# A fused GRU, attention, conditioned attention and expert network on one core: a second bank for the query-key product, a second bank for turned rows, and two pieces of a step in another order

## The reference

```python
xn = _rms_norm(x, g_norm) * (1.0 + scale) + shift      # scale, shift from emb @ W_emb
qkv = xn @ W_qkv                                       # 256 -> 3 x 256
q, k, v = ...                                          # 16 heads of 16
q, k = _rms_norm(q, g_q), _rms_norm(k, g_k)            # over each head's 16 numbers
logits = einsum('bhqd,bhkd->bhqk', q, k) * d ** (-0.5)
attn = softmax(logits)
o = einsum('bhqk,bhkd->bhqd', attn, v)
return o + o @ W_out
```

## Time and profile before

| | us |
|---|---|
| time of three runs, median | 1084.39 |
| lowest and highest | 1083.53, 1085.08 |
| the profiled execution's own time | 1083.47 |
| its span in the trace | 1081.3 |

### The profile page before, as it was taken

One profiled execution on the slowest core, in us unless ns is written; L12 is line 12 of the kernel. 1 busy time (PEld: TensorE's weight loads), 2 busy tenths in 40 slices (PEclk: granted clock), 3 DMA queues, 4 the chain that ended last, 5 costly groups with the idle time before them and its releaser, 6 DMA issues. The chain is left out here.

```text
span 1081.3 us, 33994 instructions
## 1 busy us (share of the span) xinstructions
PE 951.9 (88%) x13386; PEld 674.3 (62%) x13386; DVE 666.0 (62%) x2544; ACT 546.5 (51%) x1792; POOL 539.6 (50%) x1245
## 2 busy tenths in 40 slices
PE   3989999999999998679999999576985999999997
PEld 3777777777777777548888887444444444444443
DVE  5866666666666666677777777746855445454554
ACT  4544444444444444447777777566762333333432
POOL 1266666666666666615555553285002555555551
PEclk8555555555555555579999999988997999999999
DMA  6100000000000000020000100100000111112111
GB/s 267 42 4 4 3 4 3 4 3 3 4 4 3 4 3 4 2 81 31 31 31 31 31 2 2 35 3 2 1 1 18 35 60 58 51 51 68 51 51 39
DMA packets 9017, 30.28 MB, mean 28 GB/s; under 512 B 1446, under 2 KB 3112, under 8 KB 8492
## 3 DMA queue, kind: packets, MB, share of 16 engines
q1 hardware_dynamic: 8876, 28.32, 7.8%
HBM read 27.27 MB, written 1.05 MB: 26 GB/s over the span
## 5 line engine op out<-in xcount | busy, mean ns | idle before, releaser
L423 POOL COPY gp<-hq 128x16 f16<-128x16 f16 x256 | 69.1, 270 | 174.5 <-DVE hq L413 174.5
L306 ACT ACTIVATE r_scan<-gr 128x8 f32<-128x8 f32 x256 | 46.6, 182 | 180.3 <-PE gr L218 180.3
L432 POOL TENSOR_TENSOR q_part<-q_raw,q_part 128x64 f16<-128x64 f32 x238 | 111.6, 469 | 19.2
L398 DVE TENSOR_REDUCE z_sum<-gz 128x8 f32<-128x16 f32 x256 | 44.8, 175 | 120.6 <-PE gz L218 120.0
L218 PEld LDWEIGHTS gr<-hq,w_two 128*128 128x128 f16 x1024 | 47.4, 107 | 115.0 <-DVE hq L408 109.9
L218 PE MATMUL gr<-hq,w_one 128*128 128x4 f16 x2048 | 117.6, 166 | 0.0
L273 PE MATMUL gq<-gp,wq_part 128*128 128x64 f16 x1428 | 114.4, 237 | 0.0
L218 PE MATMUL gr<-hq,w_two 128*128 128x4 f16 x1024 | 68.7, 171 | 51.6 <-DVE hq L408 28.8
L924 POOL TENSOR_SCALAR probs<-probs,rinv 128x128 f32<-128x128 f32 (+1 forms) x128 | 53.0, 427 | 119.5 <-DVE rinv L820 119.5
L430 POOL CAST q_part<-q_raw 128x64 f16<-128x64 f32 x238 | 108.6, 456 | 0.0
L218 PEld LDWEIGHTS gr<-hq,w_one 128*128 128x128 f16 x2048 | 94.1, 103 | 0.0
(11 more groups left out here) (257 smaller groups left out, 2687.8 us busy)
## 6 DMA issues: line engine op xcount, KB each, us to landing
wf_ffn<-in_wf SPq DMA_DIRECT2D x28, 448.0 KB, 3.3
raw_attn<-in_pairs SPq DMA_DIRECT2D x8, 770.0 KB, 4.4
shared<-in_wq SPq DMA_DIRECT2D x1, 2056.0 KB, 12.3
xT<-in_xT SPq DMA_DIRECT2D x1, 1024.0 KB, 7.7
x<-in_xr SPq DMA_DIRECT2D x1, 1024.0 KB, 6.6
out<-fin SPq DMA_DIRECT2D x4, 256.0 KB, 2.5
whh<-in_whh SPq DMA_DIRECT2D x1, 768.0 KB, 4.7
wih<-in_wih SPq DMA_DIRECT2D x1, 768.0 KB, 6.8
```

The source lines that it names most:

```text
L306: nc.scalar.activation(r_scan[:, 2::3], R[bp][:, k * 8:(k + 1) * 8], ACT.Sigmoid, scale=1.0 / GS).then_inc(t_in, 1)
L398: nc.vector.tensor_reduce(z_sum[:], Z[bp][:, k * 16:(k + 1) * 16] .rearrange("p (m q) -> p m q", q=2), AX.X, ALU.add).then_inc(z_sum_ready, 1)
L423: nc.gpsimd.tensor_copy(gp[:, :, :, :, t].rearrange("p q j b -> p q (j b)"), hq[:, nxt, :, 2::3]).then_inc(h_stored, 1)
L432: nc.gpsimd.tensor_tensor(q_part[:, 1, h, :, :, c], src, q_part[:, 0, h, :, :, c], ALU.subtract).then_inc(q_split, 1)
```

## The change

It does four things, all in `adaln_block`.

1. The query-key product alternates between two banks (`qk_banks`), odd tiles in the old one, even tiles in `other32`. The product of tile t waits for `qk_ready` of tile t - 2.
2. A second bank for turned rows, `turn[1]`, which is the same memory as `other32`, is used alternately with `turn[0]` from the q rows of tile 6 to the k rows of tile 7, that is k rows of tile 6 and q rows of tile 7. After that it is the fifth bank for scores and weights.
3. Scores and weights therefore have 3 banks in turn in steps 4 to 7, 4 in steps 8 and 9 (`v_bank` is added), and 5 from step 10 on.
4. On TensorE `values` stands ahead of `batch_product`; and the shifted rows of a batch's second tile are turned (TensorE) and copied (ScalarE) after the first of a step's two units, not at the step's end.

```diff
-        bk = [... nc.psum_tensor(f"cb{i}", [P, HALF], F32) for i in range(7)]
-        turn = ctx.enter_context(nc.psum_tensor("turn", [P, 2 * HALF], FP16))
-        v_bank, x_bank, qk_bank = bk[4], bk[5], bk[6]
+        free_bank = [... for i in range(3)]
+        v_bank, x_bank, qk_bank = [... for i in range(3, 6)]
+        turn = [ctx.enter_context(nc.psum_tensor(f"turn{i}", [P, 2 * HALF], FP16)) for i in range(2)]
+        turn32, other32 = turn[0][:].bitcast(F32), turn[1][:].bitcast(F32)
+        qk_banks = (other32, qk_bank)
+        bk = free_bank + [v_bank, other32]
...
-            at = n % 4 if t < C0 else n % 5
+            at = n % (3 if t < TILES else 4 if t < TILES + 2 else 5)
...
+        two = [turn_of["q", TILES - 2], turn_of["k", TILES - 1]]
+        last_turn = [None, None]
+        for n, use in enumerate(turns):
+            at = (n - two[0]) % 2 if two[0] <= n <= two[1] else 0
+            turn_bank[use], turn_before[use], last_turn[at] = turn[at], last_turn[at], n
...
             def free_turn(kind, n):
-                at = turn_of[kind, n]
-                if at:
-                    pe.wait_ge(turn_read, at)
+                if turn_before[kind, n] is not None:
+                    pe.wait_ge(turn_read, turn_before[kind, n] + 1)
+                elif turn_bank[kind, n] is turn[1]:
+                    pe.wait_ge(qk_ready, TILES - 1)
...
             def freed(kind, n):
+                at = place[kind, n]
                 if before[kind, n]:
                     kind, n = before[kind, n]
                     pe.wait_ge(mx_done if kind == "score" else exp_done, n + 1)
+                elif at == 3:
+                    pe.wait_ge(v_done, TILES)
+                elif at == 4:
+                    pe.wait_ge(turn_read, last_turn[1] + 1)
...
-                    if t:
-                        pe.wait_ge(qk_ready, t)
-                    projected(qk_bank[:], t, slice(0, 2 * D), qk_psum)
+                    if t >= 2:
+                        pe.wait_ge(qk_ready, t - 1)
+                    projected(qk_banks[t % 2], t, slice(0, 2 * D), qk_psum)
...
                     if n == 0:
-                        if ("y", t // 4 - 3) in turn_of and t % 4 == 3 and t >= 15:
-                            batch_product(t // 4 - 3)
                         if 1 <= g <= QUADS:
                             values(g - 1)
+                        if t % 4 == 3 and t >= 15:
+                            batch_product(t // 4 - 3)
+                        b = (t - S0 - 4) // 4
+                        if t % 4 == 0 and 0 <= b < B:
+                            pe.wait_ge(shift_lo, b * TC + 2)
+                            rows_turned("shifted", q_rows, b * TC + 1)
...
-                b = (t - S0 - 4) // 4
-                if t % 4 == 0 and 0 <= b < B:
-                    pe.wait_ge(shift_lo, b * TC + 2)
-                    rows_turned("shifted", q_rows, b * TC + 1)
...
                     if n == 0 and 1 <= g <= QUADS:
                         raw(g - 1)
+                    b = (t - S0 - 4) // 4
+                    if n == 0 and t % 4 == 0 and 0 <= b < B:
+                        rows("shifted", qT, b * TC + 1)
```

More of the change, by code:

```diff
@@ L1021, in adaln_block @@
         oT = sb("oT2", [P, J, NT])
-        bk = [ctx.enter_context(nc.psum_tensor(f"cb{i}", [P, HALF], F32)) for i in range(7)]
-        turn = ctx.enter_context(nc.psum_tensor("turn", [P, 2 * HALF], FP16))
-        turn32 = turn[:].bitcast(F32)
-        v_bank, x_bank, qk_bank = bk[4], bk[5], bk[6]
+        free_bank = [ctx.enter_context(nc.psum_tensor(f"cb{i}", [P, HALF], F32))[:] for i in range(3)]
+        v_bank, x_bank, qk_bank = [ctx.enter_context(nc.psum_tensor(f"cb{i}", [P, HALF], F32))[:]
+                                   for i in range(3, 6)]
+        turn = [ctx.enter_context(nc.psum_tensor(f"turn{i}", [P, 2 * HALF], FP16)) for i in range(2)]
+        turn32, other32 = turn[0][:].bitcast(F32), turn[1][:].bitcast(F32)
+        qk_banks = (other32, qk_bank)
+        bk = free_bank + [v_bank, other32]
         o_bank = (x_bank, qk_bank)
@@ L1069, in weights_at @@
             return n if 0 <= n < len(weight_units) else None
-        uses, bank, before = [], {}, {}
+        uses, bank, place, before = [], {}, {}, {}
         for t in range(STEPS):
@@ L1078, in adaln_block @@
         for n, (kind, unit, t) in enumerate(uses):
-            at = n % 4 if t < C0 else n % 5
-            bank[kind, unit], before[kind, unit], last[at] = bk[at], last[at], (kind, unit)
-        turns = []
+            at = n % (3 if t < TILES else 4 if t < TILES + 2 else 5)
+            bank[kind, unit], place[kind, unit] = bk[at], at
+            before[kind, unit], last[at] = last[at], (kind, unit)
+        turns, turn_bank, turn_before = [], {}, {}
         for t in range(STEPS):
@@ L1129, in rows_turned @@
                 for hp in range(HP):
-                    mm = pe.transpose(turn[:, hp * P:(hp + 1) * P],
+                    mm = pe.transpose(turn_bank[kind, i][:, hp * P:(hp + 1) * P],
                                       rows[:, i, 2 * hp:2 * hp + 2, :].rearrange("p h n -> p (h n)"),
@@ L1262, in rows @@
                 nc.scalar.activation(dst[:, :, tile_cols(i)],
-                                     turn[:].rearrange("p (h t) -> p h t", h=HP),
+                                     turn_bank[kind, i][:].rearrange("p (h t) -> p h t", h=HP),
                                      ACT.Copy).then_inc(turn_read, 1)
@@ L1278, in exponentials @@
                     nc.scalar.activation(pT[:, n // 2 % 2, n % 2 * 2 + e].rearrange("p k t -> p (k t)"),
-                                         bank["weight", 2 * n + e][:], ACT.Exp,
+                                         bank["weight", 2 * n + e], ACT.Exp,
                                          scale=scale).then_inc(exp_done, 1)
@@ L1304, in _ @@
                         act.wait_ge(ss2_ready, t)
-                    nc.scalar.activation(sq[:], qk_bank[:], ACT.Square).then_inc(sq_ready, 1)
+                    nc.scalar.activation(sq[:], qk_banks[t % 2], ACT.Square).then_inc(sq_ready, 1)
                 if 2 <= t < TILES + 2:
@@ L1326, in _ @@
                     rows("shifted", qT, b * TC)
-                b = (t - S0 - 4) // 4
-                if t % 4 == 0 and 0 <= b < B:
-                    rows("shifted", qT, b * TC + 1)
         @block.vector
@@ L1340, in maximum @@
                 nc.vector.tensor_reduce(mx[:, i, 4 * q + e:4 * q + e + 3:2],
-                                        bank["score", 2 * n + e][:]
+                                        bank["score", 2 * n + e]
                                         .rearrange("p (c t) -> p c t", c=2),
@@ L1404, in _ @@
                     dve.wait_ge(rstd2_ready, t + 1)
-                    nc.vector.tensor_tensor(heads_of(qk[:, t % 2]), heads_of(qk_bank[:]),
+                    nc.vector.tensor_tensor(heads_of(qk[:, t % 2]), heads_of(qk_banks[t % 2]),
                                             rstd2[:, t, :].unsqueeze(2).to_broadcast([P, 2 * H2, DH2]),
```

## The result

| | before | changed |
|---|---|---|
| median, us | 1084.39 | 1079.18 |
| lowest and highest of 7 runs each | 1083.53, 1086.08 | 1076.69, 1081.46 |
| profiled execution, us | 1083.47 | 1079.19 |
| its span, us | 1081.3 | 1077.1 |

The ratio is 0.9947, 95% interval [0.993, 0.9964]: about 0.5% faster. The forecast was 1077.6 with a range of 1074.4 to 1081.0.

A forecast was written before the change was run, and what follows sets the result against it. Tile rounds and steps 8 and 9 were taken as bound by chains, not an engine. 4.0 + 1.55 + 1.25 = 6.8 us off 1083.47 gives 1076.7, with 0.9 added a median of 1077.6; range 1074.4 to 1081.0.

The forecast's parts named there:

- rival (b): Clock falls before the turnings of steps 7 to 9: 2.3 us, not 4.0; 5.1 in all, 1079.3 us; chance 0.19.
- Part 1: Tile rounds: two banks for the query-key product remove a wait; 0.45 us in rounds 0 to 3, 1.45 by tile 7.
- Part 2: Three score banks, steps 4 to 7: hidden until step 7, where 0.55 us is lost; bounds 0 and 0.7.
- Part 3: Steps 7 to 9: two banks for turned rows; turnings to first weights 5.8 us instead of 10.8, a gain of 5.0.
- The wait in the bank table: Step 10: the first weight must wait for the maximum of step 9's last score half, about 1 us.
- my single case: Steps 8 to 10: turnings at full clock, then half from about 746.7; Parts 1 to 3 give 4.0 us; chance 0.47.
- rival (a): Clock stays at 1.00 through steps 8 to 10: 5.9 us in place of 4.0, 8.7 in all, 1075.7; chance 0.18.
- Part 4: Steps 15, 19 and 23: `values` ahead of y covers y's wait for `oT`; 0.55, 0.55 and 0.45, 1.55 us.
- part 5: Steps 12, 16, 20: second tile's shifted rows turned mid-step; 0.42 us of a 1.12 us wait gained, three times, 1.25 us.
- Rival (c): Later steps: ScalarE is what is late, so part 5 costs 2.8 us; 2.75 in all, 1081.6; chance 0.08.
- Rival (d): Tile rounds: TensorE pauses more often and its clock stays at 0.50; five rounds make 9.7 us more, 1094; chance 0.04.

The follow-up runs named there:

- the second profile: The changed kernel measured again without any edit: 1078.5 us, ratio 0.9956; its profiled execution took 1076.57 us.
- Run 5: The changed kernel with 12 extra matmuls into a free score bank in step 2, to keep TensorE busy: 1077.49 us, ratio 0.9932.
- run 4: The changed kernel with every query-key product in one bank, waiting for the multiplication of the tile before: 1079.19 us, ratio 0.9945.
- run 7: The changed kernel with one product bank and four score banks in steps 4 to 7: 1078.61 us, ratio 0.9947.
- run 3: The changed kernel with every turning in `turn[0]`, one bank for turned rows as before: 1084.78 us, ratio 1.0002.
- run 6: The changed kernel with 12 extra matmuls in step 2, 4 ahead of tile 6's q rows and 10 in step 9: 1075.6 us, ratio 0.9919.
- run 1: The kernel before with the two edits of order alone (`values` ahead of y, second tile's shifted rows in mid-step): 1082.47 us, ratio 0.9974.

## Why the prediction was right, and where it was not

**The sum.** 6.8 us were forecast, 5.81 measured inside the block and 5.2 between the medians. In the second profile it was 6.61 inside the block and 1083.47 - 1076.57 = 6.9 in time. The range held, and each part worked by the mechanism named; two sizes and the clock were off. Some of the agreement is luck. The median of 1079.18 is nearer to rival (b)'s 1079.3 than to the forecast's 1077.6, and of the 2.5 us between the profiled 1079.19 and the 1076.7 forecast for it 1.47 are the block's later start, of which the prediction said nothing. The sizes:

**Part 1** (0.45 us by tile 4, 1.45 by tile 7) was too high: 0.15 and 0.86 in the first profile, 0.51 and 1.22 in the second. The reasons were the ones given, `x_lo` and product 2 at half clock, and rounds 2 and 3 averaged 4.4 us where 4.3 were forecast. Run 5 gave the upper bound its size: 25.10 - 23.53 = 1.57 us by tile 4 where I had 1.7.

**Part 2** (0.55 us lost at the shifted rows of tile 0) was the term most off: 0.91 in both profiles (0.86 gained at tile 7, -0.05 left, and 1.22 to 0.31), and 0.96 between runs 4 and 7. It was outside my bound of 0.7. The rows of step 7, the first from the kernel before and the other two from the changed one, show where it goes:

```profile
741.49 0.61 PE L1150 MATMUL cb<-kT,qT 64*128 64x256 f16 x8
...
742.17 0.61 PE L1166 MATMUL cb<-kT,qT 64*128 64x256 f16 x6
743.35 0.39 PE L1166 MATMUL cb<-kT,qT 64*128 64x256 f16 x2 [0.57 <-DVE mx L1356]
```

From the first scores to the turning were 742.15 - 741.49 = 0.66 us and are 743.67 - 742.17 = 1.50. My bound was the length of one maximum; TensorE idles 0.57 us for it, and the last score pair then stands by itself in front of the turning. So the second product bank and the three score banks that it forces nearly cancel at the shifted rows of tile 0: 41.39 before, 41.44 and 41.08 with both, 41.27 in run 7 with neither. Run 7's median of 1078.61 is not told apart from the changed kernel's.

**Part 3** (10.8 us to 5.8) was right: 6.90 with half the turnings at 1.2 GHz, 6.01 at full clock. It carries the gain of the banks; run 3 without it is no faster than before, though 0.8 us of that is the clock. The wait in the bank table was put at about 1 us and was 1.00 to 1.21 us.

**The clock** was the right thing to be unsure of, and my single case was too simple. I let it fall after the turnings. In the first profile it fell within them, in the wait for the first copy that rival (b) names, but rose again before the fifth; in the second it fell behind them. So the first profile lies between the forecast and rival (b): 5.81 us in the block, where the one had 6.8 and the other 5.1. At the first weights the gain was 3.86 us against 5.9 forecast: 0.6 less from part 1, 0.35 from part 2, 0.9 from the clock in the turnings, and 0.2 because they took 6.01 us at full clock and not 5.8. In the second it was 5.11. Half clock and bank wait up to the first values took 0.9 and 1.1 us of it where I had put 1.9 with the small pieces, so that parts 1 to 3 gave 2.99 and 4.02 us against 4.0. The 4.02 is two misses that cancel: 0.8 too much forecast up to the first weights and 0.8 too much loss behind them. Full clock through steps 8 to 10, rival (a), came in neither profile, but with the extra matmuls of run 6.

**Part 4** (1.55 us) measured 0.63 + 0.56 + 0.53 = 1.72 and **part 5** (1.25 us) 0.37 + 0.31 + 0.43 = 1.11, read as the steps in the gain from one `values` to the next. The sum of 2.8 us was met in the changed kernel and in run 1. Rival (c) fell: the wait that part 5 removes (1.12 us, of which 0.27 stay) was longer than what the delay takes of it. By the strict order of ScalarE's queue (the Trainium skill, PSUM — Partial Sum Buffer, "Engine vs sequencer instructions") the last exponentials of step 16 stand behind the copy; the trace agrees, with the copy at 780.75 and the exponentials at 781.65. Rival (d), a clock that stays low through the rounds, did not come: rounds 4 to 6 ran at 1.00.

## What to carry to other kernels

When two engines hand one buffer back and forth, a second buffer is worth the most where every use waits for a copy and nothing else; where another input is due soon after, it gives little, and if it is taken from a pool that was just large enough, the pool's new wait can take all of it back. Count the price at the place where the waiting instruction has the critical one behind it. After a chain is shortened, look at TensorE's granted clock in the stretch: here half clock behind idle time cost 1.4 us in product 2 and 1.9 us around the first values, and extra matmuls into a free bank bought it back (runs 5 and 6). Compare two profiles only where the clock was the same in both: against one profile of the changed kernel the second product bank looked worthless, against the other it was worth 0.7 us.

## What was not expected of the hardware

The same kernel took 1076.6 to 1082.1 us. TensorE's clock has a part in it: between the two profiles of the changed kernel it made 0.9 us in the turnings alone. In the block's tail it was at full speed in the changed kernel and part of the time at half in run 4, whose instructions there are the same:

```profile
810.60:816.70 6.10, 4.11 (x30) 2.42 (x30) 1.24 (x4) 0.38 (x1) 0.00 (x0) 1.00 0.01 3
...
809.40:817.60 8.20, 6.21 (x30) 3.67 (x30) 1.24 (x5) 0.38 (x1) 0.00 (x0) 0.68 0.01 2
```

From the last values to the last addition were 6.1 us in the one and 8.2 in the other; what made the clock fall there in some executions and not in others stays open. Groups of eight turnings followed the clock as matmuls do: 0.61 us at a granted clock of 1.00, 1.01 at 0.50. Extra work on TensorE, 26 matmuls of 128x512, made the kernel 3 us faster.
